# Nine-stage transformer kernel: GpSimd adds the two feature halves ahead of the layer norms' partition sums, and TensorE sums with one matmul in place of two

## What is computed

```
def _layernorm(x, axis=-1, eps=1e-05):
    m = jnp.mean(x, axis=axis, keepdims=True)
    v = jnp.var(x, axis=axis, keepdims=True)
    return (x - m) / jnp.sqrt(v + eps)

x = x + mamba(_layernorm(x))                 # state-space scan
x = x + moe0(_layernorm(x))                  # 8 experts, top 2, shared expert
x = x + rotary_attention(_layernorm(x))
x = x + moe0(_layernorm(x))
x = x + gated(latent_attention, pattern_attention)(_layernorm(x))
x = x + moe1(_layernorm(x))                  # 16 experts, top 4, shared expert
x = x + grouped_attention(_layernorm(x))
x = x + moe1(_layernorm(x))
```

## Time and profile before

| what | value |
|---|---|
| median of 3 runs | 4443.25 us (4432.36 to 4448.92) |
| the profiled execution, its own time | 4442.63 us |
| its span (first to last instruction) | 4440.8 us |
| busy: PE, DVE, ACT, POOL | 86%, 58%, 38%, 31% |
| mean granted TensorE clock | 0.924 |

### The profile page before, as it was taken

How to read it: one execution, slowest core, us unless ns; L and a number is a source line. 1 busy time by engine, 2 the same in 40 slices (tenths; PEclk the granted TensorE clock), 3 DMA queues, 4 the chain that set the end, 5 groups by cost and what they waited for, 6 DMA issues and landing times. The chain is left out here.

```text
span 4440.8 us, 45564 instructions
## 1 busy us (share of the span) xinstructions
PE 3833.4 (86%) x16352; PEld 2484.6 (56%) x16352; DVE 2591.0 (58%) x4355; ACT 1674.7 (38%) x2870; POOL 1357.2 (31%) x1074
## 2 busy tenths in 40 slices
PE   5879878887988886988888979999888888889999
PEld 4557644445844434555555547788644444467887
DVE  5655466665456656777777756333376676664333
ACT  2423256653235541333333223222245555532222
POOL 3234322214320114232323324443321221144442
PEclk8889989998989977999999989999889999989999
DMA  2000000001000002000000010000000000010000
GB/s 74 1 22 21 14 1 1 1 1 47 13 7 5 5 22 78 24 20 24 20 24 20 24 52 21 25 26 15 18 1 1 1 1 1 6 42 21 26 9 19
DMA packets 32909, 83.35 MB, mean 19 GB/s; under 512 B 6320, under 2 KB 7472, under 8 KB 32304
## 3 DMA queue, kind: packets, MB, share of 16 engines
q1 hardware_dynamic: 32688, 80.44, 6.0%
HBM read 59.44 MB, written 4.19 MB: 14 GB/s over the span
## 5 line engine op out<-in xcount | busy, mean ns | idle before, releaser
L1174 DVE TENSOR_REDUCE max_cols<-ps 128x1 fp32r<-128x512 f32 x1024 | 637.0, 681 | 288.3 <-PE ps L1104 287.5
L1149 ACT ACTIVATE probs<-ps 128x512 f32<-128x512 f32 x1024 | 546.9, 603 | 253.4 <-PE ps L1113 156.8
L768 POOL TENSOR_TENSOR h_lo<-h,h_hi 128x512 fp32r<-128x512 f32 x304 | 392.3, 1291 | 817.8 <-ACT h_hi L853 817.8
L932 DVE TENSOR_TENSOR gated<-silu,ps 128x512 f32<-128x512 f32 x288 | 198.2, 688 | 679.8 <-PE ps L235 666.1
L847 ACT ACTIVATE silu<-ps 128x512 f32<-128x512 f32 x304 | 181.8, 598 | 896.8 <-PE ps L235 896.7
L233 PE MATMUL ps<-xn_hi,w_hi 128*128 128x512 f32 x1216 | 483.7, 398 | 0.0
L234 PE MATMUL ps<-xn_lo,w_hi 128*128 128x512 f32 x1216 | 477.7, 393 | 0.0
L235 PE MATMUL ps<-xn_hi,w_lo 128*128 128x512 f32 x1216 | 476.9, 392 | 0.0
L338 POOL CAST o_hi<-o_scaled 128x512 fp32r<-128x512 f32 x64 | 39.1, 611 | 907.4 <-DVE o_scaled L1196 907.4
L1119 PE MATMUL ps<-probs,v_aug 128*32 128x512 f32 x2048 | 308.5, 678 | 0.0
L233 PEld LDWEIGHTS ps<-xn_hi,w_hi 128*128 128x128 f32 x1216 | 232.3, 191 | 51.6 <-issue 3.1
(11 more groups left out here) (462 smaller groups left out, 7898.5 us busy)
## 6 DMA issues: line engine op xcount, KB each, us to landing
raw<-in_w_ffn SPq DMA_DIRECT2D x76, 448.0 KB, 3.3
raw<-raw SPq DMA_DIRECT2D x256, 64.0 KB, 2.0
composed_inputs<-in_m_latent SPq DMA_DIRECT2D x2, 2560.0 KB, 9.7
raw<-in_w_mamba SPq DMA_DIRECT2D x8, 448.0 KB, 6.0
raw<-in_w_latent SPq DMA_DIRECT2D x5, 448.0 KB, 6.6
x<-in_x SPq DMA_DIRECT2D x4, 512.0 KB, 6.5
gated_pattern<-gated SPq DMA_DIRECT2D x4, 512.0 KB, 3.4
raw<-gated_pattern SPq DMA_DIRECT2D x4, 512.0 KB, 4.2
```

Source lines behind the costliest of these rows:

```text
L768: nc.gpsimd.tensor_tensor(HL[:, b % 3, :], hb[:, b % 2, :], HH[:, b % 3, :].bitcast(F32), ALU.subtract).then_inc(G.sem, G.step((s, ev)))
L932: nc.vector.tensor_tensor(ga if routed(i) else hb[:, i % 2, :], sg[:, i % 2, :], bank[2 + i % 2], ALU.mult).then_inc(V.sem, V.step((s, "ga ...
L1149: nc.scalar.activation(self.PB[:, n % 8, :], self.scores(n), ACT.Exp, scale=self.scale).then_inc(A.sem, A.step((s, ("exp", n))))
L1174: nc.vector.tensor_reduce(self.MB[:, self.tile_of(g, h) % 2, q, col:col + 1], self.psum(ev), op=ALU.max, axis=AX.X, negate=True).then_inc( ...
```

## The change

`x_halves` is a new buffer of 128 x 512. Ahead of each mean GpSimd writes the sum of the two halves of `x` into it, and TensorE multiplies it once. For the chunks 1 to 3 GpSimd also adds the halves of `sq` in place ahead of var; for chunk 0 VectorE does. The sum for chunk 0 of a stage is made at the end of the stage before, as soon as the chunk's last addition to `x` is done (`x_done`); that for chunk `b` + 1 stands on GpSimd right behind xn cut `b` (in latent behind the scale event), in the ffn stages and mamba thus ahead of the pieces of the weights that are cut next. In latent, `dev` shares the new buffer, and var and dev of chunks 1 to 3 come one place later.

```diff
+        x_halves = sb("x_halves", [P, L])
...
             def pool(pool, s):
+                add_x_halves(pool, s, 0)
                 stage_start(pool, s)
...
+        def add_x_halves(pool, s, b):
+
+            if b:
+                pool.wait_ge(PE.sem, PE.at((s, ("mean", b - 1))))
+            elif s:
+                pool.wait_ge(V.sem, V.at(stages[s - 1]["x_done"](s - 1)))
+                pool.wait_ge(PE.sem, PE.at((s - 1, ("mean", NB - 1))))
+            if s == 0:
+                pool.wait_ge(x_in[b], 16)
+            nc.gpsimd.tensor_tensor(x_halves[:, :], x[:, 0, b * L:(b + 1) * L], x[:, 1, b * L:(b + 1) * L],
+                                    ALU.add).then_inc(G.sem, G.step((s, ("x halves", b))))
+
+        def add_square_halves(pool, s, b, sq):
+
+            pool.wait_ge(A.sem, A.at((s, ("squared", b))))
+            nc.gpsimd.tensor_tensor(sq[:, 0, :], sq[:, 0, :], sq[:, 1, :], ALU.add).then_inc(G.sem, G.step((s, ("square halves", b))))
+
+        def add_first_square_halves(dve, s, sq):
+
+            dve.wait_ge(A.sem, A.at((s, ("squared", 0))))
+            nc.vector.tensor_tensor(sq[:, 0, :], sq[:, 0, :], sq[:, 1, :], ALU.add).then_inc(V.sem, V.step((s, ("square halves", 0))))
+
         def front_pe(pe, s, ev, psum, sq):
 
             kind, b = ev[:2]
-            for k in range(KD):
-                of = x[:, k, b * L:(b + 1) * L] if kind == "mean" else sq[:, k, :]
-                last = nc.tensor.matmul(psum, c256[:, :], of, start=k == 0, stop=k == KD - 1)
-            return last
+            if kind == "mean":
+                pe.wait_ge(G.sem, G.at((s, ("x halves", b))))
+            else:
+                added = G if b else V
+                pe.wait_ge(added.sem, added.at((s, ("square halves", b))))
+            return nc.tensor.matmul(psum, c256[:, :], x_halves[:, :] if kind == "mean" else sq[:, 0, :], start=True, stop=True)
...
             elif kind == "var":
+                if b == 0:
+                    add_first_square_halves(dve, s, sq)
                 dve.wait_ge(PE.sem, PE.at((s, ev)))
                 nc.vector.transpose(sq[:, 0, :], psum).then_inc(V.sem, V.step((s, ev)))
...
                         cut(pool, s, ev, XH[:, :, b * L:(b + 1) * L], XL[:, :, b * L:(b + 1) * L], xc[:, :, :],
                             [(V, V.at((s, ("xn", b))))])
+                        if b + 1 < NB:
+                            add_x_halves(pool, s, b + 1)
                         if b == 0:
                             for t in range(1, gt):
                                 piece(t)
+                    elif kind == "squared" and b:
+                        add_square_halves(pool, s, b, sq)
...
-            dev = alloc("dev", [P, L])[:, :]
+            dev = x_halves[:, :]
...
-                    put(g + 4, 1, ("var", b + 1))
-                    put(g + 4, 2, ("dev", b + 1))
+                    put(g + 4, 2, ("var", b + 1))
+                    put(g + 4, 3, ("dev", b + 1))
...
+                    elif kind == "tokens" and ev[1] + 1 < NB:
+                        pool.wait_ge(V.sem, V.at((s, ("scale", ev[1]))))
+                        add_x_halves(pool, s, ev[1] + 1)
```

More of the change, by code:

```diff
@@ L466, in pe @@
                     if kind in ("mean", "var"):
-                        if kind == "mean":
-                            pe.wait_ge(x_in[b], 16)
-                        else:
-                            pe.wait_ge(A.sem, A.at((s, ("squared", b))))
                         front_pe(pe, s, ev, psum(ev), sq).then_inc(PE.sem, PE.step((s, ev)))
@@ L778, in pe @@
                     if kind in ("mean", "var"):
-                        if kind == "var":
-                            pe.wait_ge(A.sem, A.at((s, ("squared", b))))
                         front_pe(pe, s, ev, ROUTE, sq).then_inc(PE.sem, PE.step((s, ev)))
@@ L943, in vec @@
                                                 ps[3][:, :, :], ALU.add).then_inc(V.sem, V.step((s, ev)))
-            return {"sync": sync, "pool": pool, "pe": pe, "act": act, "vec": vec, "pieces": nt}
+            return {"sync": sync, "pool": pool, "pe": pe, "act": act, "vec": vec, "x_done": lambda s: (s, ("added", (NG - 1) * NB * gt + gt - 1)),
+                    "pieces": nt}
         AUXB = (3, 4, 5, 7)
@@ L1293, in pe @@
                     heads.free(s, ev, by_act, by_vec)
-                    if kind == "var":
-                        by_act.append((s, ("squared", b)))
-                    elif kind == "qk":
+                    if kind == "qk":
                         pe.wait_ge(G.sem, G.at((s, ("xq cut" if ev[2] < 2 else "xkv cut", b))))
@@ L1560, in pe @@
                     heads.free(s, ev, by_act, by_vec)
-                    if kind == "var":
-                        by_act.append((s, ("squared", b)))
-                    elif kind in ("qk", "v", "gate"):
+                    if kind in ("qk", "v", "gate"):
                         pe.wait_ge(G.sem, G.at((s, ("xn cut", b))))
@@ L1625, in pool @@
                         cut(pool, s, ev, XH[:, :, :], XL[:, :, :], xc[:, :, :], before)
+                        if b + 1 < NB:
+                            add_x_halves(pool, s, b + 1)
+                    elif ev[0] == "squared" and ev[1]:
+                        add_square_halves(pool, s, ev[1], sq)
             def vec(dve, s):
@@ L1870, in pool @@
                             cut_pieces(pool, d1[ahead(s):], first[s] + ahead(s))
+                    elif kind == "tokens" and ev[1] + 1 < NB:
+                        pool.wait_ge(V.sem, V.at((s, ("scale", ev[1]))))
+                        add_x_halves(pool, s, ev[1] + 1)
+                    elif kind == "squared" and ev[1]:
+                        add_square_halves(pool, s, ev[1], sq)
                     elif kind == "mid squared":
@@ L1889, in pe @@
                         (by_act if reader[old[0]] is A else by_vec).append((s, old))
-                    if kind == "var":
-                        by_act.append((s, ("squared", ev[1])))
-                    elif kind == "composed":
+                    if kind == "composed":
                         n = ev[1]
@@ L1942, in pe @@
                     last = None
-                    if kind == "mean":
-                        for k in range(KD):
-                            last = nc.tensor.matmul(bank[slot(ev)], c256[:, :], x[:, k, ev[1] * L:(ev[1] + 1) * L],
-                                                    start=k == 0, stop=k == KD - 1)
-                    elif kind == "var":
-                        for k in range(KD):
-                            last = nc.tensor.matmul(bank[slot(ev)], c256[:, :], sq[:, k, :], start=k == 0, stop=k == KD - 1)
+                    if kind in ("mean", "var"):
+                        last = front_pe(pe, s, ev, bank[slot(ev)], sq)
                     elif kind == "mid":
@@ L2248, in vec @@
                                                 ALU.add).then_inc(V.sem, V.step((s, ev)))
-            return {"sync": sync, "pool": pool, "pe": pe, "act": act, "vec": vec, "pieces": npieces, "ahead": send_ahead}
+            return {"sync": sync, "pool": pool, "pe": pe, "act": act, "vec": vec, "x_done": lambda s: (s, ("scale", NB - 1)),
+                    "pieces": npieces, "ahead": send_ahead}
         def grouped():
@@ L2334, in pe @@
                     heads.free(s, ev, by_act, by_vec)
-                    if kind == "var":
-                        by_act.append((s, ("squared", b)))
-                    elif kind in ("qk", "v"):
+                    if kind in ("qk", "v"):
                         pe.wait_ge(G.sem, G.at((s, ("xn cut", b))))
```

22 lines of the change are left out of this document (18 added, 4 removed).

## The result

| what | before | after |
|---|---|---|
| median | 4444.62 us (4432.36 to 4452.4, 10 runs) | 4458.94 us (4440.38 to 4466.98, 10 runs) |
| ratio to before | | 1.0029, interval 1.0015 to 1.0043 |
| profiled execution, its span | 4442.63, 4440.8 | 4440.38, 4438.4 |
| mean granted clock, all runs | 0.921 to 0.930 | 0.911 to 0.916 |

The change makes the kernel slower by 14 us or 0.29%. By the bound of 0.5% that is no difference; the interval lies above 1 all the same, the forecast of 4411 missed by 48 us, and the time lies outside the range of 4388 to 4442. The clock of before is that of its runs beside all experiments. Two executions of the kernel before beside the last three experiments took 7131.22 and 9803.21 us, far outside all others, and are left out of every figure here.

What follows compares the result with a forecast made beforehand. TensorE, busy 86% of the span, was taken as the bound. Terms 15.5 + 10.8 + 2.6 - 3 + 11.6 + 2.7 - 4.7 - 3 gave 32.5 us gained: 4411 us, range 4388 to 4442.

Steps and rivals of the forecast that it cites:

- means and vars inside the ffn stages: Five shorter means and vars in each of four ffn stages: 15.5 us gained, range 10.3 to 17.2.
- Clock: Rival: with less to do TensorE gets the half level more often, which eats the gain: 4443 us, chance 0.06.
- Starts of stages: Shorter first norms: 11.6 us gained at ffn and grouped-size terms aside, mamba 2.7 gained, attention starts 4.7 lost, latent nothing.
- 1.0 each, 3.9: Var 0 at the four ffn starts: 1.72 saved at the half level, less VectorE's sum and a hop.
- 1.1 each, 4.4: Mean 1 at the four ffn starts: 0.6 us late behind its queued sum, but 1.72 shorter.
- 4.7 lost in rotary, pattern and grouped: At these starts VectorE's sum comes behind its clearing: 2.1 us lost in rotary and pattern each, 0.5 in grouped.
- Inside rotary, pattern, grouped: 18 means and vars, 15.5 us at full clock; taken at 0.7: 10.8 us gained, range 4.7 to 15.5.
- Absorbed: Rival: the savings end in waits for VectorE and ScalarE, some 14 us gained, 4429 us, chance 0.21.
- mamba inside: Var waits for GpSimd's sum and VectorE's additions may stretch: 3 us lost, range 0 to 6.
- Latent: Inside latent, six means and vars worth 5.2 us, half of it taken: 2.6 us gained.
- Port: Rival: each GpSimd sum inside stages stops VectorE for its whole length: 34 us slower, 4477 us, chance 0.09.
- signs of failure: Ffn gains under 3 us each; slower L607, L332 and routing; clock below 0.91; sum-caused idle ahead of var over 15 us.

Runs made afterwards that it cites:

- drop_ffn0: Kernel before with the second matmul of each mean and var dropped in the two ffn0 stages alone, 16 of 72, no sums added: 4442.76 us, ratio 1.0001.
- sum_first: Kernel after with VectorE's sum of the first squares issued ahead of its memset in rotary, pattern and grouped: 4446.52 us, ratio 1.0005.
- drop_only: Kernel before with the second matmul of every mean and var left out (half of the features), nothing added: 4422.01 us, ratio 0.9951.
- adds_only: Kernel after with both matmuls of each mean and var kept and the sums made into a buffer no matmul reads: 4459.85 us, ratio 1.0036.
- after_twice: Kernel after with the one matmul of each mean and var done twice on the same sum: 4488.1 us, ratio 1.0098.
- first_var_two: Kernel after with the first var of each stage done by two matmuls again and VectorE's sum gone: 4445.99 us, ratio 1.0009.
- var_only: On the kernel after: means and each stage's first var keep two matmuls without sums, other vars use GpSimd's sum and one: 4439.06 us, ratio 0.9992.
- mean_only: On the kernel after: only means use GpSimd's sum and one matmul, every var has two matmuls and no sum: 4445.67 us, ratio 1.0007.
- late_stages: On the kernel after: sums and single matmuls in the last three stages alone, first var of each with two matmuls: 4445.28 us, ratio 1.0004.
- drop_fill: Kernel before without the second matmuls, plus six filler matmuls ahead of vars 2 and 3 in the two ffn0 stages: 4409.97 us, ratio 0.9929.

## Why the prediction was wrong

**The step that failed first** is "20 x 0.86 = 17.2 us. ... I take 0.9 of it: 15.5 us" for means and vars inside the ffn stages. I saw the 12 waits for the routing there and took them for a loss of a tenth. By the table, less the starts, the ffn1 stages gained 2.9 and 2.1 us inside and the ffn0 stages lost 3.7 and 3.6: 2.2 us lost in all, 17.7 off. It is more, since the forecast counts the shorter mean 1 (4 x 1.72 = 6.9 us) under the starts, while the table's start ends where mean 1 begins: 22.4 gained was forecast for the same stretch, so 24.6 off. `drop_ffn0` shows the cause for ffn0: the gain is nil even with no sum anywhere. Part ends in the longer waits (1.91 for 1.49, 2.96 for 2.47), which I had thought of, and part in falls of the clock behind them, which I had given to the rival *Clock* with 0.06. My argument against that rival, that the share of work hardly changes, looked at the mean over the kernel; the falls come at single places, and three in a stage are enough.

**Starts of stages**: "1.0 each, 3.9", "1.1 each, 4.4", "11.6 us", mamba 2.7, and 4.7 lost in rotary, pattern and grouped, so 9.6 gained. The profile has 2.5 gained in the ffn starts, 0.7 in mamba and 10.5 lost in the three attention starts (6.4, 3.4, 0.7): 7.3 lost. Without mean 1's shortening the forecast for this was 2.8 gained, so 10.1 off. For the attention starts the direction was right and the size was not: I had counted the sum's own length behind the memset and a stretch of it to 2.07. It was GpSimd that was stretched, from 2.08 to 6.28 us, and the weights with it. `sum_first` puts some 12 us on that order alone.

**Inside rotary, pattern, grouped** (10.8) can't be judged from one execution, since equal code differed by 10.8 us in rotary. One reading behind the term was wrong. The two groups of the earlier trace rows were compared as if at one clock, but in before the group with the norm ran at 1.00 and the one without at 0.92:

```profile
1482.37:1506.30 23.93, 21.15 (x101) 10.03 (x102) 17.81 (x31) 14.92 (x25) 5.31 (x4) 1.00 0.00 0
1576.06:1598.37 22.31, 18.42 (x93) 9.59 (x94) 13.89 (x24) 10.93 (x22) 1.89 (x2) 0.92 0.00 1
```

At 0.92 over 22.31 us some 1.8 us of the second are the clock's, so by this estimate the 3.44 us of norm matmuls cost some 3.4 there and not 1.62. The pair does not speak for *Absorbed*. In after, pattern's group with the norm takes 24.29 us where 22.7 was forecast for 23.93:

```profile
1495.06:1519.35 24.29, 20.95 (x97) 10.18 (x98) 17.46 (x31) 15.25 (x25) 6.58 (x5) 0.93 0.00 1
```

At a clock of 0.93 over 24.29 us, 3.4 us ran at the half level, so some 1.7 us are the clock's. Without the fall it would be 22.6: the matmuls were saved, and the fall took it.

**Right**: the price (0.86 and 1.71 us, the chain above); mamba inside, forecast 3 lost, 2.2 lost (its three vars wait 7.5 us longer, and six matmuls save 5.2); GpSimd's busy time, 81 us forecast, 89.7 found, of which 2 x 4.2 are the two blocked subtractions. **Latent**, 2.6 forecast, 0.2. **Port**: VectorE is busy 31 us longer, 6 of them its nine sums, but the rival as I put it (a VectorE stop of 1.29 us for each of 54 sums, the kernel 34 us slower) did not happen. On the mean L607 takes 1042 ns for 1033 and L332 873 for 863, and `drop_only`, with no sum at all, already has 9 us of the 31. What happened is a stop of GpSimd, at the starts of the attention stages.

Of my signs of failure two held: the ffn stages gain less than 3 us each but for one, and idle time put down to GpSimd's square sums is 31.3 us. The second held for the wrong reason, since 23.3 of that stood there before; the growth is 8 us, nearly all in mamba. The clock went to 0.912 and not below the 0.91 I had named, a bound that was set too low to see it. The two steps, off by 24.6 and 10.1, are read from the profiled execution, which is 2.4 us quicker than that of before and has a pattern stage 9.8 us shorter; the 17 us between that and the medians' difference of 14.3 are assigned to no stage.

## What to carry to other kernels

Ahead of paying for less TensorE work, run the kernel with that work simply left out: here the free version gave 22 us of 62, and 72 sums could not be had for that. Price each removed matmul by what stands behind it: where the next thing is a wait for another engine it is worth nothing, and may cost clock; where TensorE runs through, as in ffn1, it is worth about its full time. Before two stretches of a trace are compared, read the granted clock of both. When one VectorE instruction with two SBUF inputs is added, put it ahead of a long memset, not behind it.

## What was not expected of the hardware

**A queued VectorE instruction blocks GpSimd during the one ahead of it.** In rotary and pattern, in after, `adds_only` and `after_twice`, a sum of two SBUF inputs stood right behind the 3.47 us memset, and in all six cases one GpSimd instruction running in the memset's time ended only behind it and the sum: in after 6.28 and 6.27 us for 2.08; in `adds_only` and `after_twice` a copy of 0.82 us took 3.85 to 3.87. Here `adds_only` in rotary:

```profile
532.02 3.47 DVE L1203 MEMSET v_aug<- 128x4096 f32 x1 [0.80 <-issue]
532.87 3.85 POOL L224 CAST w_rotary_hi<-raw 128x768 fp32r<-128x768 f32 x1
535.41 0.63 DVE L323 TENSOR_TENSOR dev<-sq 128x512 f32<-128x512 f32 x1
```

The stop lasts until the sum ends: in after the extra 4.20 us are the memset and the sum together, and in `adds_only` 0.68 us of the copy's 0.82 still follow the sum's end at 536.04. Grouped shows it in the same three kernels beside its 1.76 us memset (2.97 us for 0.93, twice 2.38 for 0.50). In before and the five others that I looked at (`sum_first`, `first_var_two`, `var_only`, `mean_only`, `late_stages`), where the transpose out of PSUM stands behind it, none of twelve memsets held GpSimd up (1.80 us during it in the earlier trace rows). The Trainium skill (SBUF — State Buffer, SBUF: two separate sides, and Who interferes with whom in it) has a GpSimd instruction that reads SBUF and a VectorE instruction with two SBUF inputs lock the shared ports for the whole instruction, and one with at most one SBUF input, outside the two-port modes, leave them free. By that the memset alone would not stop GpSimd, and it doesn't; the rows fit the page if the lock is taken while the sum still waits for the memset to end. That reading is inferred from the twelve and the six and was not tried by itself.

**Less work, lower clock.** `drop_only` lies at 0.914 to 0.917, the kernel before at 0.922 to 0.929, and `drop_fill`, with six fillers, at 0.918 to 0.922 and 12 us lower. Equal code shows the same link from one execution to the next: rotary's 490.5 us at 0.89 and 501.3 at 0.87.
